# Output projections of four batches as three float32r parts, low parts of the gated rows on GpSimd

## What is computed

```python
def _L0_ffn_ref(x, w_gate, w_up, w_down):
    h = silu(x @ w_gate) * (x @ w_up)
    return sparsify_2to4(h) @ w_down        # of every 4 neighbours the 2 largest stay
...
def _L0_attn_ref(x, norm_w, W_skip, W_in, conv_w, conv_b, Wd1, Wd2, bd2, WB, WC, A_log, W_D, W_out):
    xn = x * rsqrt(mean(x * x) + EPS) * norm_w
    skip = xn @ W_skip.T
    u = silu(causal_conv4(xn @ W_in.T) + conv_b)
    delta = softplus(u @ Wd1.T @ Wd2.T + bd2)
    Bt, Ct = u @ WB.T, u @ WC.T
    # scan over the 512 tokens, for 1024 channels x 16 states:
    # h = exp(delta * A) * h + (delta * u) * Bt ;  y = sum over the states of h * Ct
    y = (y + u * W_D) * silu(skip)
    return y @ W_out.T
x = x + 0.5 * ffn(layernorm(x)); x = x + mamba(layernorm(x)); x = x + 0.5 * ffn(layernorm(x))
```

## Time and profile before

| | |
|---|---|
| time, median of 3 runs | 3476.42 us (3474.21 to 3479.85) |
| the profiled execution: time | 3474.36 us |
| the profiled execution: span of the core | 3472.4 us |
| PE busy | 3339.7 us (96%) |
| DVE busy | 3001.2 us (86%) |
| POOL busy | 2586.3 us (74%) |
| ACT busy | 2001.8 us (58%) |
| DMA | 696.44 MB, mean 201 GB/s |

### The profile page before, as it was taken

How to read it: one execution, slowest core, us unless ns; L and a number is a source line. 1 busy time by engine, 2 the same in 40 slices (tenths; PEclk the granted TensorE clock), 3 DMA queues, 4 the chain that set the end, 5 groups by cost and what they waited for, 6 DMA issues and landing times. The chain is left out here.

```text
span 3472.4 us, 38888 instructions
## 1 busy us (share of the span) xinstructions
PE 3339.7 (96%) x12020; PEld 2111.1 (61%) x12020; DVE 3001.2 (86%) x3549; ACT 2001.8 (58%) x2762; POOL 2586.3 (74%) x1625
## 2 busy tenths in 40 slices
PE   8999999999999999999999999999999899999899
PEld 6776656556656665556656565557555565555467
DVE  5645998789889899999989999999999998999934
ACT  5545657557565674666655675667565575554322
POOL 1314876667787778878788889888989988989813
PEclk9999999999999999999999999999999999999999
DMA  9656566656757566567666675657646566556433
GB/s 364 226 197 191 163 213 214 230 171 213 238 179 230 173 230 233 155 218 226 206 209 206 196 233 200 194 188 233 232 146 213 178 212 204 188 161 200 136 111 113
DMA packets 243469, 696.44 MB, mean 201 GB/s; under 512 B 23536, under 2 KB 23792, under 8 KB 233584
## 3 DMA queue, kind: packets, MB, share of 16 engines
q1 hardware_dynamic: 173632, 559.72, 46.6%
q10 hardware_dynamic: 69632, 134.23, 15.1%
HBM read 619.94 MB, written 76.55 MB: 201 GB/s over the span
## 5 line engine op out<-in xcount | busy, mean ns | idle before, releaser
L1476 POOL TENSOR_TENSOR scan_in<-du,scan_rows 128x512 f32<-128x512 f32 x1024 | 1312.5, 1297 | 561.2 <-DVE decay L1349 491.8
L1349 DVE TENSOR_TENSOR_SCAN decay<-decay,scan_in 128x512 f32<-128x512 f32 x1024 | 1247.9, 1221 | 13.3 <-POOL scan_in L1476 7.5
L1489 POOL TENSOR_TENSOR y<-y,scan_out 128x1024 f32<-128x1024 f32 x512 | 1222.5, 2388 | 0.3 <-DVE scan_out L1359 0.3
L928 ACT ACTIVATE decay<-delta,small 128x512 f32<-128x512 f32 x1024 | 698.4, 688 | 887.3 <-DVE scan_out L1359 881.7
L692 PE MATMUL side<-zhi,wunit 128*128 128x512 f32 x2048 | 907.1, 443 | 12.9 <-DVE res_g L1334 2.9
L693 PE MATMUL side<-zhi,wunit 128*128 128x512 f32 x2048 | 814.3, 398 | 0.0
L784 PE MATMUL side<-h,wdown 128*128 128x512 f32 x1760 | 798.9, 598 | 8.9 <-DVE res_r L1334 4.0
L1359 DVE TENSOR_TENSOR scan_out<-decay,scan_rows 128x512 f32<-128x512 f32 x1024 | 700.8, 685 | 29.9 <-POOL y L1489 7.2
L697 PE MATMUL side<-zlo,wunit 128*128 128x512 f32 x2048 | 565.7, 397 | 1.9 <-DVE zlo L1253 0.9
L784 PEld LDWEIGHTS side<-h,wdown 128*128 128x128 f32 x1760 | 333.5, 191 | 379.9 <-issue 346.8
L915 ACT ACT_TABLE_LOAD x409 | 524.7, 1283 | 7.7 <-DMA bc_dram<-cv 0.5
(11 more groups left out here) (110 smaller groups left out, 2884.2 us busy)
## 6 DMA issues: line engine op xcount, KB each, us to landing
wunit<-hl_dram SPq DMA_DIRECT2D x480, 512.0 KB, 4.2
scan_rows<-bc_dram ACTq DMA_DIRECT2D x256, 512.0 KB, 5.7
wdown<-down_w_dram SPq DMA_DIRECT2D x256, 256.0 KB, 3.2
wmam<-mam_dram SPq DMA_DIRECT2D x128, 512.0 KB, 4.2
hl_dram<-wunit SPq DMA_DIRECT2D x32, 512.0 KB, 5.8
delta<-skip_dram SPq DMA_DIRECT2D x16, 1024.0 KB, 7.2
wmam<-wout_dram SPq DMA_DIRECT2D x32, 512.0 KB, 4.4
skip_dram<-dts SPq DMA_DIRECT2D x56, 256.0 KB, 4.9
```

The lines of the kernel that those rows point to most:

```text
L928: nc.scalar.activation(decay[u % BANKS][:], delta[:, e, :], ACT.Exp, scale=aneg[:, e * N + n:e * N + n + 1]).then_inc(sem["decay_ready"], 1)
L1349: nc.vector.tensor_tensor_scan(decay[u % BANKS][:], decay[u % BANKS][:], db[u % INPUTS][:], 0.0, ALU.mult, ALU.add).then_inc(sem["state_re ...
L1476: nc.gpsimd.tensor_tensor(db[u % INPUTS][:], du[:, e, :], rows[m % ROWS][:, 0, :], ALU.mult).then_inc(sem["input_ready"], 1)
L1489: nc.gpsimd.tensor_tensor(y[:, e:e + 2, :], y[:, e:e + 2, :], scan_out[:, k:k + 2, :], ALU.add).then_inc(sem["sum_ready"], 1)
```

## The change

The 32 `out` jobs of batches 0 to 3 become three-part float32r jobs of 12 matmuls; those of batches 4 to 7 stay. For that:

- in the head SP loads W_out raw (2 MB, one DMA), ACT and DVE split it in eight pieces on ticks 11, 13, ... 25, and SP stores each piece (512 KB) to HBM;
- one tick behind each of the eight gates ACT copies the four gated tiles as high parts (`yhi`, in the place of `delta`) and POOL subtracts them for the low parts (`ylo`, in place of `y`), behind its unit work of that tick;
- the jobs begin two ticks behind the gate (`OUT_LATE`), half 1's `dl`, `first` and `du` of the next batch and its projections move by a tick too; each job loads its own 512 KB weight tile, four for a half where it were two;
- at least six units are dealt by the fourth tick of a half;
- the tables are other numbers: five more pauses in all (at product 45 where they were at 37, none but single ones until 236), and batches start up to four ticks earlier, the first and the last at the same ticks.

```diff
+SPLIT_OUTS = 4
+OUT_LATE = (1,) * SPLIT_OUTS + (0,) * (8 - SPLIT_OUTS)
...
-PAUSES = {0: 9, 37: 6, 176: 1, 204: 1, 224: 4, 388: 1, 412: 1, 444: 4, 480: 28}
+PAUSES = {0: 9, 45: 4, 100: 1, 116: 1, 168: 1, 236: 5, 452: 6, 480: 33}
...
-STARTS = (67, 128, 189, 250, 312, 360, 409, 453, 516)
+STARTS = (67, 125, 187, 248, 311, 356, 409, 452, 516)
...
-            after = max(self.middle[b] + 3, self.project_end[b + 1] + 1) if b < B - 1 else self.middle[b] + 3
+            after = self.middle[b] + 3 + OUT_LATE[b]
+            if b < B - 1:
+                after = max(after, self.project_end[b + 1] + 1)
+            last = STARTS[b + 1] + 3 + OUT_LATE[b]
...
+                loads += [(self.out_at[b, half] + t + 0.1, ("out", b, half, t), ("out", b, half, t)) for t in range(KD if b < SPLIT_OUTS else 0)]
...
+            sp.dma_start(raw_out[:], out_raw).then_inc(sem["out_raw_loaded"], 16)
             sp.dma_start(wdt_dram, wdt_in).then_inc(sem["mam_copied"], 16)
...
+                w = split_out_of(tick - 1)
+                if w is not None:
+                    sp.wait_ge(sem["out_part_ready"], w + 1)
+                    sp.dma_start(out_dram[w], out_parts[:, w % HE].bitcast(f32)).then_inc(sem["out_part_stored"], 16)
...
+            def project_split_out(key):
+                _, b, half, t = key
+                bank = side_bank(key)
+                w = weights(key)
+                for e in range(HE * half, HE * half + HE):
+                    pe.wait_ge(sem["out_high_ready"], KE * b + e + 1)
+                    nc.tensor.matmul(bank[:], w[:, e % HE, :], yhi[:, e, :], start=(e % HE == 0), stop=False)
+                    nc.tensor.matmul(bank[:], w[:, HE + e % HE, :], yhi[:, e, :], start=False, stop=False)
+                for e in range(HE * half, HE * half + HE):
+                    pe.wait_ge(sem["out_low_ready"], KE * b + e + 1)
+                    mm = nc.tensor.matmul(bank[:], w[:, e % HE, :], ylo[:, e, :], start=False, stop=(e % HE == HE - 1))
+                mm.then_inc(sem["side_ready"], 1)
...
+            def gated_high(b, half):
+                act.wait_ge(sem["gated_ready"], HE * (2 * b + half + 1))
+                for e in range(HE):
+                    nc.scalar.activation(yhi[:, HE * half + e, :], y[:, HE * half + e, :], ACT.Copy).then_inc(sem["out_high_ready"], 1)
...
+            def gated_low(b, half):
+                for e in range(HE):
+                    pool.wait_ge(sem["out_high_ready"], HE * (2 * b + half) + e + 1)
+                    nc.gpsimd.tensor_tensor(ylo[:, HE * half + e, :], y[:, HE * half + e, :], yhi[:, HE * half + e, :],
+                                            ALU.subtract).then_inc(sem["out_low_ready"], 1)
```

80 lines of the change are left out of this document (60 added, 20 removed).

## The result

The changed kernel takes 3485.86 us (median of 7 runs, 3482.42 to 3489.13), the kernel before in the same session 3476.22 (7 runs, 3472.18 to 3479.85): ratio 1.0030, 95% interval 1.0018 to 1.0042. It is slower by 10 us, where I forecast no change and a range of 3456 to 3492. The profiled execution spans 3484.1 us against 3472.4.

What follows compares the result with a forecast made beforehand. PE was taken to bound 482.80 to 1891.81 us, DVE 2432.80 to 3295.20. Stretches -11, head DMAs +6, reload of `u` +3 and new chain +2 sum to 0: 3476 us on the median's scale, range 3456 to 3492.

Steps and rivals of the forecast that it cites:

- the sum by stretches: Whole kernel: job differences between batch starts and middles, priced on the engine that binds each stretch, sum to -11 us.
- the reload of `u`: Loading the next batch's `u` before `dt`: late by 3.6 us at batch 3 and 2.3 at batch 4; +3 us taken.
- POOL's queue: Subtractions on POOL at eight gates hold back later inputs; DVE stalls 0 to 5 us at six gates; 0 taken.
- The head: Ticks 0 to 67: +9 us for more PE work and +6 us for products delayed by full DMA engines.
- The saving on PE: Ticks 97 to 312: 28 `out` jobs, 2 products and 4 `win` fewer take 25.3 us off PE; -24 us taken.
- each stretch moves with the engine that binds it: Rule for every stretch: its length changes with the priced work of its binding engine, PE or DVE.
- The sign that I had named: In `scan`, waits for `scan_in` of 20 us and more in total would show the starved scan to be right.
- The new chain: Copies and subtractions behind a gate: PE waits 4 us for low parts at batch 2, half 1; +2 us taken.
- Ticks 67 to 97: This stretch, ending at tick 96 in the new plan: PE -4.9 us, DVE -2.6 us of work; -3 us taken.
- Ticks 384 to 516: The last long stretch, from tick 382 in the new plan: 2 us more on DVE; +2 us taken.
- POOL starves the scan: Rival: subtraction blocks make DVE late at gates, so PE stops; 3488 to 3494 us, slower; chance 0.28.
- The stalls are covered: Rival: new waits fall where an engine waits anyway; 3456 to 3471 us, likeliest 3464; chance 0.34.

Runs made afterwards that it cites:

- plan alone: Changed kernel with the output jobs of all batches in float32, no W_out split and no subtractions, new tables and later ticks kept: 3495.81 us (1.0053).

## Why the prediction was wrong

Two steps failed, at about equal cost. The first is the sum by stretches, with the later tick at nothing beyond the reload of `u`: its terms make the plan in float32 11.5 us slower (-11 without the form's 19.5, and +3), and it came out 20.5 us slower (14 to 23). The second is POOL's queue, set at 0: leaving the subtractions out of the changed kernel gives 8.8 us back. That the total missed by only 10 us is in part luck, since the rows of the sum missed by -8.4 and -4.3 us in two stretches and by +12.6, +8.2 and +3.5 in three others.

- **The head** (+9 and +6) was right in its sum: +14.5. Of these 2.2 are the start of product 0 and belong to no change, 4.7 the DMAs' where I took 6, and 7.6 the work's where I took 9. The plan alone shows the same, a head of 311.7 us with product 0 at 22.5 (+7.5). Loading and splitting W_out later gives some 3.4 back.
- **The saving on PE** came to 20.2 us of busy time in ticks 97 to 312, where I had 25.3 with all that moved, and ticks 360 to 384 grew by 14.8 (forecast 13). What failed is the rule "each stretch moves with the engine that binds it": PE's idle time in the third stretch rose by 13.8 us. With the subtractions left out on the new tables that stretch lasts 1396.7 us, so 5.9 of the miss of 12.6 are the subtractions' and 6.7 remain. These are the plan's: in float32 the stretch lasts 1413.1 us, 4.1 more than before, where my terms without the form give 4 less, and PE's idle time is already 20.2 us.
- **POOL's queue** (0, bounds 0 and 20): 9 us on the new tables, 27 on those of before. The working pointed the right way (next input 7.7 us behind the gate at best, DVE with three or four units in hand), and its own result, a stall of 0 to 5 us at six gates, was then set at nothing because DVE has 10% to spare in the mean. At a gate it can have none: on the tables of before its late `h` then stops PE for 6.76 us. I also looked only at `scan_in`; the ring that binds is the other one, `scan_out`, freed by POOL's sums. The sign that I had named, waits for `scan_in` of 20 us, didn't come (9.0), while the waits for sums are 16.1 us against 3.3 without subtractions.
- **The new chain** (+2): PE never waited for a low part. That it waited 4.54 us at the very place that I had named is luck: 4.09 us of it are there without subtractions and 4.10 in float32. It comes from DVE's row of work and from the pauses, which leave PE no product there.
- **The reload of u** (+3): 1.1 us at batch 3 and 0.5 at batch 4, against 3.6 and 2.3. At batch 3 the load was issued 0.7 us behind the last job where I had 1.8, it landed 8.3 us later where I had 8.7, and PE took 7.9 us for the work between where I had 6.9.
- **The tick itself** was no term of the sum. I priced what the tick does to half 0; with half 1's, and the floor of six units, it was worth some 13 us in float32 on the tables of before. There the stretch of ticks 97 to 312 grows from 1406.9 to 1416.2 us, so the plan's cost in that stretch on the new tables is of the same size, though no run takes the tick out there. It was in the diff: next projections a tick later, right behind jobs that hold their buffers.
- **Ticks 67 to 97** (-3): -11.4, and -11.1 in the plan alone. PE's busy time fell by 8.9 us where I had 4.9, and PE and DVE idle less as well. I have no account of that; it went my way by luck.
- **Ticks 384 to 516** (+2): +10.2. DVE is busy 10.3 us more. Some 3.5 of these are a scan, a compare and a read more in the stretch (958 instructions, 955 before). The other 6.9 are instructions that take longer: `zlo` 1133 ns in the mean where it was 932, the gate 3243 where it was 3004, `du` 4970 where it was 4221. The plan alone, in float32, shows the same length from tick 382 to the first product behind tick 516 (902.5 us, 902.8 in the changed kernel, 893.8 before from tick 384), so it is the new order of work and not the form. The traces show that these are the instructions that meet POOL's. Two `du` of the changed kernel, the first with POOL idle, the second beside its inputs and a sum:

```profile
2946.74 2.29 DVE L1471 TENSOR_TENSOR du<-delta,du 128x2048 f32<-128x2048 f32 x1 [1.46 <-ACT y L1202]
...
3047.96 5.70 DVE L1471 TENSOR_TENSOR du<-delta,du 128x2048 f32<-128x2048 f32 x1
3049.09 2.42 POOL L1565 TENSOR_TENSOR y<-y,scan_out 128x1024 f32<-128x1024 f32 x1
```

In both kernels every gate and `du` without a record of POOL beside it takes 2.28 to 2.29 us and every such `zlo` 0.68 to 0.69. In this stretch the three kinds overlap POOL's records by 18.7 us before and 25.8 now, which is the 6.9 us.
- **The rivals.** "POOL starves the scan" named the mechanism of the second step and 3488 to 3494; it came to 3486, but only 9 us are POOL's and the plan makes up the rest. "The stalls are covered" had its reason (a late step of one engine seldom meets a late step of another) refuted: at seven of eight gates PE came out later.

What stays open is how much of the plan's cost on the new tables is the tick's and how much the tables' own (11 us in float32), and what in the old tables made exactly three gates of eight bad.

Of the kernels here that compute the whole result, only the one that starts batch 1 a tick earlier beat the kernel before, by 0.1%. The bound without subtractions and without the later tick (3464.64 against 3474.12 in its session) shows what the form is worth with least against it: 9.5 of the 19.5 us. It is a bound and no kernel, as the low parts are missing from its result.

## What to carry to other kernels

A block of work that must wait for an event, put in the row of an engine that feeds a ring, costs its waiting time as well as its own: count the idle time in front of it, and count each ring that this engine fills or frees. Spare time of an engine in the mean is no cover next to an event at which it is already late. A wait that stands where you forecast one need not be yours: look for it in the kernel without the change's new work. An engine's saving can be spent by the tick that makes room for it, so price what a shifted job now stands next to, above all whether its buffer is freed in time.

## What the runs showed of the hardware

- Waits of PE of 3.51, 4.54 and 7.99 us were each followed by matmuls at 0.63 us instead of 0.40, and by windows of 4 us with a granted clock near 0.50, then 0.64 to 0.73, then 1.00. With the slow matmuls behind it, the wait of 4.54 us costs 6.7.
- DVE's subtraction of 128 by 512 takes 0.68 us, or up to 2.87 us beside POOL; its multiply of 128 by 2048 takes 2.29 us, or up to 7.03. In ticks 384 to 516 the time added is about the time of the overlap with POOL's records. DVE's multiply `scan_out<-decay,scan_rows`, one of whose inputs lies in PSUM, takes at most 0.69 us in all 560 cases in which POOL is busy beside it from its start to its end.
- The same subtraction on POOL takes 1.24 us in a row of four (four in 4.97 to 5.02), less than the 1.44 us of the nearest row that I had taken.
- The first product starts at 22.5 to 23.1 us in 12 of the 18 traces and at 24.7 to 25.2 in the other six. The kernel doesn't decide it: the changed kernel has 24.8, the same head without subtractions 22.9. A difference of 2 us in the head is to be read with that in mind.
